# Cross attention in split float32: the weighing that opens a group of four heads moves between two value products

## The chip, the cores and the metric

The kernel runs on one core of a Trainium2 chip (trn2). The metric is the device time of one execution in microseconds (us); less is better. Engines are named as in the profile: PE is TensorE (PEld its weight loads), DVE is VectorE, ACT is ScalarE, POOL is GpSimd, SP is SyncE, which issues most of the DMAs.

## The reference

The model is six residual layers on a sequence x of 256 tokens by 512; the change touches only the first one, a cross attention of 16 heads of width 128 over a context of 4096 tokens:

```
x = x + softmax((LN(x) @ Wq) @ (ctx @ Wk).T / sqrt(128)) @ (ctx @ Wv) @ Wo     # per head, summed over heads
```

The other layers (a self attention, a small expert layer, an attention over the context, a self attention, a mixture of 64 experts) follow it and are the same code before and after.

## The kernel before, in words

Precision. Every float32 operand of the large products is split in two parts: ACT rounds it (`round_*`, a CAST to fp32r), DVE subtracts the rounded part from the original (`split_*`), and PE makes three products (hi by hi, lo by hi, hi by lo). A product's result therefore costs an ACT operation and a DVE operation, in this order, before PE can use it.

Tiling. The 4096 context tokens are 8 chunks (index j) of 512 tokens. A step (h, j) of the loops works on head h and, one head ahead, on head h+1. On PE a step has these pieces:

- K(h+1, j), `project_k`: the keys of chunk j for the next head, 12 matmuls, into bank 0.
- V(u), `project_v`: the values of 128 tokens for four heads at once (a "quad"), 12 matmuls, into one of two banks. Unit u counts all 128-token pieces of all quads; the units of quad g+1 are made during the heads of quad g. `units(h, j)` gives those of a step: none at j=0 and two at j=1 of the head that starts a quad (h = 0, 4, 8, `starts_quad`), one in every other step.
- S(h+1, j), `scores`: scores of the next head, 12 narrower matmuls into the twin bank. It waits for both key parts (`k_split`) and for the copy of the former scores out of the bank (`s_stored`).
- W(h, j), `weigh`: values weighted by the exponentials of chunk j, 8 matmuls. It waits for its values in `v_back` and for both parts of the exponentials (`e_split`). W(h, 7) is carried out in step 0 of the next head and W(h, 0) in step 1, the others one step late (W(h, j-1) at the head of step j).

Values go through DRAM: each V(u) is rounded and split into one buffer `v_out` and spilled by SP (`spill`) to `v_dram`; POOL loads the chunk that a weighing needs into the one buffer `v_back` as soon as the weighing before it is done (`load_v`). For u above 32 `round_v(u)` waits until the spill of unit u-1 has landed, because there is only the one `v_out`. `project_v(u)` waits until unit u-2 is split.

At the start of quads 4 and 8 POOL first issues two loads of the new `wv_parts` (`load_wv`), then the largest score's reduction over partitions, and then the load for W(h, 0).

Order. All engines run in the order written; each list of steps (`tensor_cross`, `scalar_cross`, `vector_cross`, `sync_cross`, `gpsimd_cross`) is written by hand. In step 1 ACT has: round exponentials, copy scores, raise scores, round values; DVE has: split exponentials, running maximum, split values, sum of exponentials. In step 2 DVE has in addition, for h above 0, a reciprocal (`invert_row`).

Late heads (h = 12, 13, 14, from `LATE`) have no value units left. Their loops are separate. In step 6 the weights wk and wq of head h+2 are rounded and split, wk first; `project_q(h+2)` runs at the end of step 7 and `project_k(h+2, 0)` after it.

Of the kernel before, what the change touches and what calls it, by code (L numbers as in the profile page):

```python
# [20 lines left out]
NCH = NKV // CH  # L21
CT = CH // P
XH, XHD = 16, 128
# [40 lines left out]
def build(nc, a, out):  # L64
    ctx = ExitStack()
    with ctx:
# [260 lines left out]
        def units(h, j):  # L327

            if h >= LATE:
                return []  # L330
            s = h % HPQ * NCH + j
            first = (h // HPQ + 1) * KVT
            return [] if s == 0 else [first, first + 1] if s == 1 else [first + s]

        def sync_cross(e):
            def load_qo(n):
                which, h = qo_order[n]
# [78 lines left out]
            for h in range(XH):  # L416
                for j in range(NCH):
                    if j == 0:
                        if h == 0:
                            e.wait_ge(q_projected, 2)  # L420
                            e.wait_ge(*v_spilled(KVT - 1))
                            load_qo(qo_order.index(("wq", 2)))
                        elif h < XH - 1:
                            e.wait_ge(q_projected, h + 2)
                            load_qo(qo_order.index(("wo", h - 1)))
                        if h == XH - 2:
                            e.dma_start(x[:], a["x"]).then_inc(x_in, 16)
                        if not has_halves(h):
                            load_wk(h + 2)
                    if j == 1 and h == XH - 1:  # L430
                        e.wait_ge(y_projected, h)
                        load_qo(qo_order.index(("wo", h)))
                    if j == NCH - 2 and has_halves(h):
                        load_wk(h + 2)
                    for u in units(h, j):
                        spill(u)
                    if j == 5 and 0 < h < XH - 1:
                        e.wait_ge(y_projected, h)
                        load_qo(qo_order.index(("wq", h + 2) if h + 2 < XH else ("wo", h)))
                    if half_at(h, j) is not None:  # L440
                        spill_half(half_at(h, j))
                    if half_at(h, j + 1) is not None:
                        load_half(h, half_at(h, j + 1))

        def tensor_cross(e):
# [135 lines left out]
            for h in range(LATE):  # L581
                for j in range(NCH):
                    if j >= 2:
                        weigh(h, j - 1)
                    elif j == 0 and h and not starts_quad(h):
                        weigh(h - 1, NCH - 1)
                    project_k(h + 1, j)
                    if j == 0 and h and starts_quad(h):
                        weigh(h - 1, NCH - 1)
                    if j == 0 and h == 0 or j == 1 and h:  # L590
                        weigh(h, 0)
                    for u in units(h, j):
                        project_v(u)
                    scores(h + 1, j)
                    if j == NCH // 2 and h:
                        finish_head(h - 1)
                    if j == NCH - 1:
                        project_q(h + 2)
# [20 lines left out]
        def scalar_cross(e):  # L619
# [127 lines left out]
            for h in range(LATE):  # L747
                for j in range(NCH):
                    if j == 0:
                        if h:  # L750
                            store_scores(h, NCH - 1)
                        round_q(h + 1)
                        round_k(h + 1, 0)
                        if h:
                            raise_scores(h, 0)
                            round_e(h, 0)
                        for u in units(h, 0):
                            round_v(u)
                        raise_scores(h, 1)
                        continue  # L760
                    if j == 1:
                        round_k(h + 1, 1)
                    round_e(h, j)
                    store_scores(h + 1, j - 1)
                    if j > 1:
                        round_k(h + 1, j)
                    if j == NCH - 1:
                        round_wk(h + 2)
                    else:
                        raise_scores(h, j + 1)  # L770
                    for u in units(h, j):
                        round_v(u)
                    if half_at(h, j) is not None:
                        round_half(half_at(h, j))
                    if j == 3 and h:
                        round_qo("wo", h - 1)
                        round_o(h - 1)
                    if j == NCH - 2:
                        round_qo("wq", h + 2)
            for h in range(LATE, XH - 1):  # L780
                store_scores(h, NCH - 1)
                round_q(h + 1)
                round_k(h + 1, 0)
                raise_scores(h, 0)
                round_e(h, 0)
                round_k(h + 1, 1)
                raise_scores(h, 1)
                round_e(h, 1)
                store_scores(h + 1, 0)
                for j in range(1, NCH):  # L790
                    if j + 1 < NCH:
                        raise_scores(h, j + 1)
                    if j > 1:
                        store_scores(h + 1, j - 1)
                    if j + 1 < NCH:
                        round_e(h, j + 1)
                        round_k(h + 1, j + 1)
                    if j == 3 and h == LATE:
                        round_qo("wo", h - 1)
                        round_o(h - 1)  # L800
                    if j + 1 == NCH - 1 and h + 2 < XH:
                        round_wk(h + 2)
                        round_qo("wq", h + 2)
            h = XH - 1
            store_scores(h, NCH - 1)
            for m in HALVES:
# [9 lines left out]
        def vector_cross(e):  # L816
# [235 lines left out]
            for h in range(LATE):  # L1052
# [17 lines left out]
                shift(h, 2)  # L1070
                split_e(h, 1)
                keep_max(h + 1, 0)
                for u in units(h, 1):
                    split_v(u)
                sum_e(h, 1)
                if half_at(h, 1) is not None:
# [1 line left out]
                for j in range(2, NCH):  # L1078
                    split_e(h, j)
                    if j == 4 and h:  # L1080
                        split_qo("wo", h - 1)
                        split_o(h - 1)
                    if j in (3, 4, 5):
                        split_k(h + 1, j)
                        shift(h, j + 1)
                    else:
                        if j + 1 < NCH:
                            shift(h, j + 1)
                        split_k(h + 1, j)
                    if j == NCH - 1:  # L1090
                        sum_e(h, j)
                        split_wk(h + 2)
                    keep_max(h + 1, j - 1)
                    for u in units(h, j):
                        split_v(u)
                    if j == 3 and h:
                        scale_o(h - 1)
                    if j < NCH - 1:
                        sum_e(h, j)
                    if half_at(h, j) is not None:  # L1100
                        split_half(half_at(h, j))
                    if j == 2 and h:
                        invert_row(h - 1)
                    if j == NCH - 2:
                        split_qo("wq", h + 2)
            for h in range(LATE, XH - 1):
# [14 lines left out]
                for j in range(1, NCH):  # L1121
                    if j + 2 < NCH:
                        shift(h, j + 2)
                    if j + 1 < NCH:
                        sum_e(h, j + 1)
                    if j in (1, 3, NCH - 2):
                        split_k(h + 1, j + 1)
                    if j == 3 and h == LATE:
                        split_qo("wo", h - 1)
                        split_o(h - 1)  # L1130
                    keep_max(h + 1, j - 1)
                    if j + 1 < NCH:
                        split_e(h, j + 1)
                        if j not in (1, 3, NCH - 2):
                            split_k(h + 1, j + 1)
                    if j == 2:
                        invert_row(h - 1)
                        scale_o(h - 1)
                    if j == 5 and h == XH - 2:
                        add_heads()  # L1140
                    if j + 1 == NCH - 1 and h + 2 < XH:
                        split_wk(h + 2)
                        split_qo("wq", h + 2)
            h = XH - 1
            keep_last_max()
            move_o(h - 1)
# [1562 lines left out]
```

## Time and profile before

| | us |
|---|---|
| median of 3 runs | 1631.89 |
| lowest, highest | 1631.61, 1635.02 |
| the profiled execution | 1632.26 |
| its span | 1630.4 |
| PE busy in it | 1595.6 (98%) |
| DVE busy in it | 1175.9 (72%) |
| ACT busy in it | 728.2 (45%) |

The span is the time from the first to the last instruction of the profiled execution. Busy matmul time counts overlapping matmuls once. A line of the timeline reads: start and duration in us, engine, source line, operation, output<-input, count, and in brackets the idle time before it with what ended it. A matmul of 512 columns follows the one before it after some 0.23 us and shows a duration of 0.39 us, so the length of a piece is best read as the distance between the starts of the first matmuls of it and of the next piece.

### The profile page before, as it was taken

What the parts mean: (1) busy time and instruction counts of PE and PEld (TensorE: products, weight loads), DVE (VectorE), ACT (ScalarE), POOL (GpSimd) and SP (SyncE); (2) the same over time, 40 slices, a digit from 0 to 9 for tenths busy, and PEclk for the clock granted to TensorE, in tenths of its full rate; (3) what the DMA queues carried; (4) which work ended last, traced back from release to release, by engine and by line L of the source; (5) the groups of instructions that cost most, each with busy time, mean ns of one, the idle gap of its engine ahead of it and who ended that gap; (6) DMA issues with size and microseconds to landing.
All of it is one profiled execution on the core that took longest, in us unless ns stands there. A gap on an engine that the chain in (4) does not pass through costs nothing. (4 is left out here: it accounts for less than half of the span.)

```text
span 1630.4 us, 23096 instructions
## 1 busy us (share of the span) xinstructions
PE 1595.6 (98%) x8798; PEld 1255.8 (77%) x8798; DVE 1175.9 (72%) x2127; ACT 728.2 (45%) x981; POOL 192.5 (12%) x247
## 2 busy tenths in 40 slices
PE   9999999999999999989999999998999999999998
PEld 7887888888788888878888888887757757544544
DVE  5555888888788888878888889999583762633333
ACT  4334554555455555544555556565331351322221
POOL 0001011010100101010110101111100071011110
PEclk9999999999999999999999999999999999999999
DMA  7876555564655655554455444334320517489994
GB/s 237 228 228 191 156 148 148 145 162 124 176 145 148 154 144 156 124 167 133 133 135 134 134 120 123 104 116 138 128 102 30 206 52 309 179 262 416 424 423 171
DMA packets 125661, 283.48 MB, mean 174 GB/s; under 512 B 7729, under 2 KB 83697, under 8 KB 119409
## 3 DMA queue, kind: packets, MB, share of 16 engines
q1 hardware_dynamic: 103248, 201.27, 38.1%
q0 software_dynamic: 22304, 80.75, 17.8%
q8 instruction: 70, 1.15, 0.3%
q14 instruction: 39, 0.31, 0.1%
HBM read 207.51 MB, written 74.48 MB: 173 GB/s over the span
## 5 line engine op out<-in xcount | busy, mean ns | idle before, releaser
L502 PE MATMUL bank<-wv_parts,cT_hi 128*128 128x512 f32 x1024 | 334.4, 390 | 1.0 <-DMA wv_parts<-wv_dram 1.0
L502 PEld LDWEIGHTS bank<-wv_parts,cT_hi 128*128 128x128 f32 x1024 | 192.8, 188 | 41.3 <-DMA wv_parts<-wv_dram 1.4
L470 PE MATMUL bank<-cT_hi,wk_hi 128*128 128x512 f32 x512 | 201.2, 393 | 0.6 <-DVE cT_lo L858 0.6
L470 PE MATMUL bank<-cT_lo,wk_hi 128*128 128x512 f32 x512 | 200.0, 391 | 0.0
L502 PE MATMUL bank<-wv_parts,cT_lo 128*128 128x512 f32 x512 | 199.8, 390 | 0.0
L470 PE MATMUL bank<-cT_hi,wk_lo 128*128 128x512 f32 x512 | 199.8, 390 | 0.0
L704 ACT CAST e_parts<-S 128x1024 fp32r<-128x1024 f32 (+1 forms) x129 | 134.9, 1045 | 139.7 <-PE bank L526 133.9
L964 DVE TENSOR_TENSOR e_parts<-S,e_parts 128x1024 fp32r<-128x1024 f32 (+1 forms) x129 | 156.0, 1209 | 40.6 <-ACT e_parts L704 37.7
L695 ACT ACTIVATE S<-S 128x1024 f32<-128x1024 f32 (+1 forms) x129 | 136.0, 1055 | 103.4 <-DVE S L930 101.3
L881 DVE TENSOR_TENSOR mx<-mx,S 128x256 f32<-128x256 f32 x390 | 165.3, 424 | 18.4 <-ACT S L689 8.1
L930 DVE TENSOR_TENSOR S<-S,mrow 128x1024 f32<-128x1024 f32 (+1 forms) x129 | 162.2, 1258 | 4.7 <-POOL mrow L1205 4.6
L953 DVE TENSOR_TENSOR esum<-esum,S 128x256 f32<-128x256 f32 x360 | 152.3, 423 | 9.5
L526 PE MATMUL bank<-e_parts,v_back 128*128 128x512 f32 x424 | 155.3, 400 | 0.0
L1192 POOL DMA_DIRECT2D v_back<-v_dram x110 | 59.0, 537 | 802.2 <-PE bank L526 776.0
L41 PE MATMUL bank<-q_hi,k_hi 128*128 128x256 f32 x512 | 145.6, 284 | 2.6 <-DVE k_lo L865 2.3
L689 ACT COPY S<-bank 128x1024 f32<-128x1024 f32 x128 | 129.3, 1011 | 36.2 <-PE bank L41 21.4
L41 PE MATMUL bank<-q_lo,k_hi 128*128 128x256 f32 x512 | 145.0, 283 | 0.0
L41 PE MATMUL bank<-q_hi,k_lo 128*128 128x256 f32 x512 | 145.0, 283 | 0.0
L673 ACT CAST k_hi<-bank 128x512 fp32r<-128x512 f32 x128 | 75.1, 587 | 151.3 <-PE bank L470 151.2
L865 DVE TENSOR_TENSOR k_lo<-bank,k_hi 128x512 fp32r<-128x512 f32 x128 | 88.2, 689 | 63.9 <-ACT k_hi L673 63.6
L525 PE MATMUL bank<-e_parts,v_back 128*128 128x256 f32 x424 | 121.2, 286 | 0.2
L470 PEld LDWEIGHTS bank<-cT_lo,wk_hi 128*128 128x128 f32 x512 | 96.2, 188 | 21.4
(328 smaller groups left out, 2793.7 us busy)
## 6 DMA issues: line engine op xcount, KB each, us to landing
w<-in_w_moe SPq DMA_DIRECT2D x32, 2304.0 KB, 15.4
v_dram<-v_out SPq DMA_DIRECT2D x112, 512.0 KB, 4.7
v_back<-v_dram POOLq DMA_DIRECT2D x110, 512.0 KB, 4.6
ctx_nat<-in_ctx SPq DMA_DIRECT2D x8, 1024.0 KB, 5.4
ctx_raw<-in_ctxT SPq DMA_DIRECT2D x7, 1024.0 KB, 8.9
v_dram<-v_back SPq DMA_DIRECT2D x14, 512.0 KB, 4.9
v_late<-v_dram POOLq DMA_DIRECT2D x14, 512.0 KB, 3.7
wv_parts<-wv_dram POOLq DMA_DIRECT2D x6, 1024.0 KB, 8.2
```

The costliest lines, as they stand in the source:

```text
L41: last = e.matmul(dst, lhs, rhs, start=(n == 0), stop=(n == len(terms) - 1))
L470: t = e.matmul(banks[b][:], l, r, start=(c == 0 and m == 0), stop=(c == DT - 1 and m == 2))
L502: t = e.matmul(banks[b][:], l, r, start=(c == 0 and m == 0), stop=(c == DT - 1 and m == 2))
L525: e.matmul(*low, start=False, stop=False)
L526: t = e.matmul(*wide, start=False, stop=(j == NCH - 1 and i == CT - 1))
L689: e.copy(S[:, j * CT:(j + 1) * CT, :].rearrange("p a t -> p (a t)"), twin[:]).then_inc(s_stored, 1)
L695: e.activation(Sj, Sj, ACT.Exp).then_inc(raised, 1)
L704: e.copy(e_place(n)[:, 0, of_chunk(0, m), :], S[:, of_chunk(j, m), :]).then_inc(e_rounded, 1)
L881: t = e.tensor_tensor(mx[:], Sj[:, 0] if first else mx[:], Sj[:, i], ALU.max)
L930: e.tensor_tensor(Sj, Sj, mrow[:].unsqueeze(1).to_broadcast([P, CT if m is None else CT // 2, T]), ALU.subtract).then_inc(shifted, 1)
L953: t = e.tensor_tensor(total, l, r, ALU.add)
L964: e.tensor_tensor(lo, S[:, of_chunk(j, m), :], hi.bitcast(F32), ALU.subtract).then_inc(e_split, 1)
```

## The change

Three edits, all in the cross attention.

At quads 4 and 8 (h = 4 and 8) W(h, 0) no longer stands before the two value units of step 1 but between them: K, V(first), W(h, 0), V(first+1), S. At h = 0, where W(0, 0) stands in step 0, the order of PE is unchanged.

At all three quad starts (h = 0, 4, 8) `moved_units` moves the rounding (ACT), the splitting (DVE) and the spill (SP) of the second unit from step 1 to step 2, ahead of those of step 2's own unit. Step 1 has then one unit on these engines and step 2 has two.

In the late heads, wq of head h+2 is rounded and split before wk of it, and in step 6 of h = 14 the last exponentials are split before the running maximum of the scores and not after it.

```diff
+        def moved_units(h, j):
+            if h < LATE and starts_quad(h) and j in (1, 2):
+                pair = units(h, 1)
+                return pair[:1] if j == 1 else pair[1:] + units(h, 2)
+            return units(h, j)
...
 # SP
-                    for u in units(h, j):
+                    for u in moved_units(h, j):
                         spill(u)
...
 # PE
-                    if j == 0 and h == 0 or j == 1 and h:
+                    if j == 0 and h == 0 or j == 1 and h and not starts_quad(h):
                         weigh(h, 0)
-                    for u in units(h, j):
+                    for n, u in enumerate(units(h, j)):
+                        if j == 1 and n == 1 and h:
+                            weigh(h, 0)
                         project_v(u)
...
 # ACT, and DVE in two places (split_v)
-                    for u in units(h, j):
+                    for u in moved_units(h, j):
                         round_v(u)
...
 # ACT, late heads (DVE the same with split_)
                     if j + 1 == NCH - 1 and h + 2 < XH:
+                        round_qo("wq", h + 2)
                         round_wk(h + 2)
-                        round_qo("wq", h + 2)
...
 # DVE, late heads
+                    if j == NCH - 2 and h == XH - 2:
+                        split_e(h, j + 1)
                     keep_max(h + 1, j - 1)
                     if j + 1 < NCH:
-                        split_e(h, j + 1)
+                        if j < NCH - 2 or h < XH - 2:
+                            split_e(h, j + 1)
```

## Rows read from the trace of the kernel before

**Rows 1.** The page, part 1: busy time, share of the span, instructions.
```profile
PE 1595.6 (98%) x8798; PEld 1255.8 (77%) x8798; DVE 1175.9 (72%) x2127; ACT 728.2 (45%) x981; POOL 192.5 (12%) x247
```
**Rows 2.** Waits of PE, 0:1130; waiter <- releaser: total us, times, longest us.
```profile
PE bank L522 <- DMA v_back<-v_dram: 6.2, 2, 3.9
PE bank L540 <- DVE esum_t L981: 3.4, 1, 3.4
...
PE bank L41 <- DVE wqo_lo L848: 1.0, 2, 0.5
...
PE bank L525 <- DVE e_parts L964: 0.6, 1, 0.6
```
**Rows 3.** Timeline of PE at the three quad starts: the idle times.
```profile
160.82 0.39 PE L41 MATMUL bank<-q_hi,k_hi 128*128 128x256 f32 x1 [1.81 <-DVE k_lo L865]
...
424.32 0.50 PE L522 MATMUL bank<-e_parts,v_back 128*128 128x512 f32 x1 [2.25 <-DMA v_back<-v_dram]
...
706.21 0.55 PE L522 MATMUL bank<-e_parts,v_back 128*128 128x512 f32 x1 [3.91 <-DMA v_back<-v_dram]
```
**Rows 4.** Windows: length, busy PE, PEld, DVE, ACT, POOL, PEclk, DMA share, GB/s.
```profile
424.00:426.00 2.00, 1.68 (x9) 1.50 (x10) 1.18 (x2) 0.00 (x0) 0.00 (x0) 1.00 0.00 0
706.00:708.70 2.70, 2.49 (x9) 2.15 (x10) 0.00 (x0) 0.00 (x0) 0.00 (x0) 0.60 0.00 0
...
1128.70:1131.00 2.30, 2.26 (x7) 1.33 (x8) 2.27 (x5) 1.33 (x4) 0.50 (x2) 0.73 0.46 98
```
**Rows 5.** Issue to landing: spills issued at 430.22, 435.29, 510.79; load at 426.31.
```profile
DMA to landing us min/median/max: 3.7/3.7/3.7
...
DMA to landing us min/median/max: 5.6/5.6/5.6
...
DMA to landing us min/median/max: 4.0/4.0/4.0
...
DMA to landing us min/median/max: 3.6/3.6/3.6
```
**Rows 6.** Timeline of PE, head 5, step 1: first matmuls of W, V, S, W.
```profile
496.82 0.39 PE L522 MATMUL bank<-e_parts,v_back 128*128 128x512 f32 x1
...
498.23 0.39 PE L502 MATMUL bank<-wv_parts,cT_hi 128*128 128x512 f32 x1
...
500.95 0.28 PE L41 MATMUL bank<-q_hi,k_hi 128*128 128x256 f32 x1
...
502.38 0.28 PE L525 MATMUL bank<-e_parts,v_back 128*128 128x256 f32 x1
```
**Rows 7.** Timeline of PE: K(5,1)'s last matmul; first of S(1,3), S(5,3), S(9,3).
```profile
421.69 0.39 PE L470 MATMUL bank<-cT_lo,wk_hi 128*128 128x512 f32 x1
...
169.22 0.28 PE L41 MATMUL bank<-q_hi,k_hi 128*128 128x256 f32 x1
...
448.31 0.28 PE L41 MATMUL bank<-q_hi,k_hi 128*128 128x256 f32 x1
...
731.84 0.28 PE L41 MATMUL bank<-q_hi,k_hi 128*128 128x256 f32 x1
```
**Rows 8.** Timeline of ACT, then of DVE, head 4, steps 1 and 2.
```profile
433.95 0.59 ACT L716 CAST v_out<-bank 128x512 fp32r<-128x512 f32 x1 [4.53 <-DMA v_dram<-v_out]
...
439.76 1.79 DVE L881 TENSOR_TENSOR mx<-mx,S 128x256 f32<-128x256 f32 x4
441.62 0.69 DVE L969 TENSOR_TENSOR v_out<-bank,v_out 128x512 fp32r<-128x512 f32 x1
...
443.94 1.75 DVE L988 RECIPROCAL esum_t<-esum_t 128x256 f32<-128x256 f32 x1
...
446.68 0.68 DVE L865 TENSOR_TENSOR k_lo<-bank,k_hi 128x512 fp32r<-128x512 f32 x1
```
**Rows 9.** The page, part 5: the group of key roundings on ACT.
```profile
L673 ACT CAST k_hi<-bank 128x512 fp32r<-128x512 f32 x128 | 75.1, 587 | 151.3 <-PE bank L470 151.2
```
**Rows 10.** Waits of DVE, 985:1128, the late heads.
```profile
DVE S L930 <- POOL mrow L1205: 1.0, 2, 0.6
```

More of the change, by code:

```diff
@@ L1072, in vector_cross @@
                 keep_max(h + 1, 0)
-                for u in units(h, 1):
+                for u in moved_units(h, 1):
                     split_v(u)
@@ L1093, in vector_cross @@
                     keep_max(h + 1, j - 1)
-                    for u in units(h, j):
+                    for u in moved_units(h, j):
                         split_v(u)
@@ L1141, in vector_cross @@
                     if j + 1 == NCH - 1 and h + 2 < XH:
+                        split_qo("wq", h + 2)
                         split_wk(h + 2)
-                        split_qo("wq", h + 2)
             h = XH - 1
```

## The prediction

> **What bounds the kernel now.** I read part 1 of the page first. PE is busy 98% of the span [rows 1], so only what PE stands idle for, or computes slowly, can be won. Next come PE's waits over the cross attention [rows 2]: 6.2 us in two waits for `v_back`, 3.4 us for `esum_t` at the end, 1.0 us in two waits for `wqo_lo`, 0.6 us for `e_parts`. The timeline of PE at the quad starts places the first two: W(4,0) at 424.32 after 2.25 us and W(8,0) at 706.21 after 3.91 us of idleness, and at h=0 S(1,2) waits 1.81 us for `k_lo` [rows 3]. So PE is the bound in heads 0 to 11, except for a few us at each quad start.
>
> The windows show a second cost. After the 3.91 us the granted clock is 0.60, a mixture of the levels 1.2 and 2.4 GHz; after the 2.25 us it is 1.00; after the 3.4 us wait for `esum_t` it is 0.73 [rows 2 to 4]. Idleness of 3.4 us lowered the clock here, 2.25 us did not. The price of one fall is read at h=8: W(8,0) takes 706.21 to 708.69 = 2.48 us against 1.41 us in head 5 [rows 3, 6], and the V behind it some 0.6 us more; 1.6 us in all is my estimate.
>
> The lengths of PE's pieces come from head 5 [rows 6]: W 498.23-496.82 = 1.41, V 500.95-498.23 = 2.72, S 502.38-500.95 = 1.43. K has 12 matmuls of V's shape: 2.72.
>
> **Part 1, W(h,0) between the two V.** PE issues no matmul more or less. At h=4, K(5,1) is issued by 421.69+0.23 = 421.92 [rows 7]. V(64) fills 421.92 to 424.64; the values landed for 424.32, so W(4,0) starts without a wait: 2.4 us less at this point. At h=8 V(96) covers 2.72 us of the wait, and the remaining 1.3 us is under the 2.25 us that left the clock alone; W(8,0) still starts at 706.21, but the V is already done and W runs at full rate. What is pushed back is load (h,1), issued behind W(h,0): 3.6 us to landing [rows 5], against V + S = 4.15 us until W(h,1), minus some 0.5 us to the issue. It just fits, as the same order does in head 5, where W(5,1) starts with no wait [rows 6].
>
> **Part 2, the second unit handled a step later.** This is where the gain can go. `v_out` is one buffer, so between the roundings of two units lies a spill's round trip. Before, it lies in step 1: ACT waits 4.53 us for it at 433.95 [rows 8], while PE has 11 us of work in that step. After, step 1 has one unit and step 2 has two, so the round trip lies in step 2, on ACT and DVE both, since DVE waits for ACT. What stands behind it on DVE is the sum, the reciprocal, the split of the exponentials, and then `k_lo` of K(5,3), for which S(5,3) waits.
>
> At h=4 step by step. PE: W(4,0) 424.64, V(65) 426.05, S(5,1) 428.77, W(4,1) 430.20, K(5,2) 431.61 to 434.33, V(66), S(5,2), W(4,2), K(5,3), V(67) to 445.3. There PE is free for S(5,3), 3 us earlier than its 448.31 before [rows 7]. DVE: `k_hi` of K(5,2) needs 0.2 us to start and 0.59 us [rows 9], so `k_lo` starts at 435.15, the maximum at 435.8, and by the distance 441.62-439.76 = 1.86 us at most (1.72 us of it is work) the split of V(65) at 437.5 and its spill at 438.2 [rows 8]. Landing: 3.7 us alone, 4.0 us where a load follows some 2 us later, 5.6 us where a load runs beside it all the way [rows 5]. Here load (4,3) is issued behind W(4,2), at about 440.4, 2.2 us later, so I take 4.0: V(66) is rounded at 442.2. From a rounding to the end of `k_lo`: 0.62 us to the DVE split, then 441.62 to 446.68+0.68 = 5.74 us [rows 8], 6.36 in all. S(5,3) can start at 448.6. Against 448.31 that is a loss of 0.3 us: the 2.4 us won in front of W(4,0) are gone, and PE now stands idle 3.2 us before S(5,3). Up to 0.2 us more may be lost at the next `k_lo`.
>
> At h=8 the same chain from 706.21 [rows 3]: V(97) 707.62, S 710.34, W 711.77, K(9,2) 713.2 to 715.9; split of V(97) 719.1, spill 719.8, next rounding 723.8, `k_lo` done 730.2. S(9,3) stood at 731.84 [rows 7]: 1.6 us won, with PE free at 727 and 3.2 us idle.
>
> At h=0 PE's order does not change. S(1,2) goes at 158.9 and loses its 1.81 us wait [rows 3]. K(1,2) ends at 156.1, V(33) is split at 159.3, spilled at 160.0, V(34) rounded at 164.0. No reciprocal (1.75 us [rows 8]) stands here, so `k_lo` comes after 6.36-1.7 = 4.7 us by DVE's work; the copy of the scores and `k_hi` [rows 9] in line on ACT make it 5.3. S(1,3) starts at 169.4 against 169.22 [rows 7]: 0.2 us lost, PE idle 2.2 us.
>
> What else moves with the unit: on SP the second spill and, behind step 2's own spill, the load of a weight half for step 3; that load starts about 1.4 us later than before (the split of V(66) goes from 441.62 [rows 8] to 442.9), while ACT takes the half up only some 7 us after its load, so nothing waits. On PE V(67) waits for the split of V(65), done at 438.2, five us before V(67) starts: no cost. POOL's queue is not touched.
>
> Sum of the quads: 0.2+0.3+0.2-1.6 = -0.9 us. The ends: with the 3.7 us landing all three are 0.3 us better (-1.8); with 5.6 us they are 1.6 us worse each (+3.9).
>
> **The clock at the new stalls.** The 3.2 us before S(5,3) and S(9,3) lie between the 2.25 us that kept the clock and the 3.4 us that lost it [rows 2 to 4]; h=0's 2.2 us is like the former. Each fall would cost 1.6 us. With even odds at each, one fall in two is the likeliest count: +1.6 us, ends 0 and +3.2. A rule stands beside this: the Trainium skill, "TensorE: Matmul & The Clock Gate", section "HAM oscillation — how this bites in real kernels", says that a wait for data long enough to make the gate fall is paid twice, in the wait and in a cold start behind it. The trace agrees at 706.21, where the clock is 0.60.
>
> **Part 3, late heads.** wq split ahead of wk gives `wqo_lo` 0.6 us earlier and ends both waits of 0.5 us [rows 2]; wk is 0.6 us later, but PE needs it only after a `project_q` and a W, 3 us on. DVE is the busier engine here; PE's 0.5 us reaches it only through POOL, which issues a load behind W before it starts the maximum: DVE waits 1.0 us for `mrow` in two waits [rows 10]. I take 0.7 us, ends 0 and 1.0. Splitting the last exponentials earlier ends the 0.6 us wait [rows 2], but PE next waits 3.4 us for `esum_t`, at the end of a DVE chain that has the same operations in another order: it waits 4.0 us instead. The clock is down there already [rows 4], so nothing changes: 0, with 0.6 us won as the other end.
>
> **Sum.** -0.9 + 1.6 - 0.7 = 0.0 us. The profiled execution took 1632.26 us, 1.86 us around its span of 1630.4; the median of the runs is 0.37 us below it. I carry the change to the median: 1631.9 us.
>
> **Rivals.**
> *No fall of the clock*: the stalls stay nearer to 2.25 us. Then -1.6 us, 1630.3. For it: the estimate of 3.2 us is below 3.4. *Both fall*: +1.6 us, 1633.5. For it: 3.2 is much nearer to 3.4 than to 2.25.
>
> *The round trip under load* (the slower side). In step 2 the spill of the second unit runs beside a value load and takes 5.6 us, as the one at 435.29 did [rows 5]. Each quad loses 1.6 us more (4.8), the stalls become 4.8, 4.8 and 3.8 us, all above 3.4, and the clock falls three times (4.8): -1.6+4.8+4.8 = +8.0, 1639.9. It decides from a landing of about 4.5 us on. Against it: the load comes 2.2 us after the spill.
>
> *The spill wait hidden* (the faster side): step 2 has enough room on DVE, PE keeps its lead and nothing stands before S(h+1,3). Then h=0 wins 1.8, h=4 2.7, h=8 2.7+0.2+1.6, the late heads 0.7: -9.7, 1622.2. For it: DVE is busy 72% only [rows 1]. Against: the second rounding would have to start 3 us earlier, before the spill it waits for has landed.
>
> **How the numbers follow.** Forecast (one fall) 0.34, no fall 0.24, both 0.20, round trip under load 0.13, spill wait hidden 0.09. A measurement of this kernel tells 0.2%, 3.3 us, from no change. Faster by more: the hidden wait and a margin of the no-fall case (quick landings, late heads at their best) for errors of my chain, 0.15. Slower by more: the loaded round trip and a part of the double fall, 0.18. Within: 0.67. The range takes in the landings between 3.7 and about 4.6 us with none to two falls: 1627.5 to 1636.5.
>
> **What would show it.** Right: no or little idleness before W(4,0), some 1.3 us before W(8,0) with the clock at 1.00 behind it; about 3.2 us of idleness before S(5,3) and S(9,3), 2.2 us before S(1,3), ended by `k_lo`; ACT waiting 4 us or more for `v_out`'s spill in step 2 and not in step 1; no wait for `wqo_lo`; a longer one for `esum_t`. Wrong: no PE wait for `k_lo` in step 3, or `v_back` still late at W(4,0), or a new wait at W(h,1).

## The result and the profile after

| | before | after |
|---|---|---|
| median, us (22 runs each) | 1632.42 | 1636.26 |
| lowest to highest, us | 1629.45 to 1635.44 | 1632.48 to 1640.45 |
| ratio of the times, 95% | | 1.0022 (1.0014 to 1.0029) |
| the profiled execution, us | 1632.26 | 1639.22 |
| its span, us, and mean granted clock | 1630.4, 0.997 | 1637.2, 0.993 |

The changed kernel is slower by 3.8 us of median, 0.14 to 0.29%. That is within my range and 4.4 us above my forecast. The runs of after differ with the clock: five took 1632.5 to 1633.3 us at a mean clock of 0.996, six took 1638.4 to 1640.5 us at 0.992 to 0.994, and the profiled one is of the last group. So its span, 6.8 us over before's, is more than the median's difference, and I read causes from its stretches, not from its total. The recorded mean clocks show how much of the loss goes with the clock: they average 0.9942 over the 22 runs of after and 0.9960 over the 66 runs of before that were timed beside the experiments. That difference times the span is 3 us, my estimate for the clock's part of the 3.8 us.

Part 1 of the page of after, against [rows 1]:

```profile
PE 1600.9 (98%) x8798; PEld 1260.9 (77%) x8798; DVE 1175.9 (72%) x2127; ACT 727.7 (44%) x981; POOL 192.6 (12%) x247
```

PE has the same number of matmuls and is busy 5.3 us longer, which goes with the lower mean clock of this execution (0.993 against 0.997). PE's waits of after over the heads of the cross attention, 0:1134, against [rows 2] (us in total, times, longest):

```profile
PE bank L41 <- DVE k_lo L874: 8.0, 3, 2.9
PE bank L547 <- DVE esum_t L990: 4.4, 1, 4.4
...
PE bank L529 <- DMA v_back<-v_dram: 1.3, 2, 0.9
```

The 6.2 us of waiting for `v_back` are 1.3, the 1.0 us for `wqo_lo` are gone, and the waits for `k_lo` are 8.0 us in three. Before had 2.3 us of them, 1.8 of it in front of S(1,2) [rows 3]; that wait is gone and the three new ones stand one step later. PE's timeline places them. W(4,0) starts with no wait, W(8,0) after 0.89 us, and S(1,3), S(5,3) and S(9,3) start after 2.25, 2.84 and 2.88 us:

```profile
169.61 0.39 PE L41 MATMUL bank<-q_hi,k_hi 128*128 128x256 f32 x1 [2.25 <-DVE k_lo L874]
...
426.60 0.39 PE L529 MATMUL bank<-e_parts,v_back 128*128 128x512 f32 x1
...
450.41 0.39 PE L41 MATMUL bank<-q_hi,k_hi 128*128 128x256 f32 x1 [2.84 <-DVE k_lo L874]
...
710.09 0.50 PE L529 MATMUL bank<-e_parts,v_back 128*128 128x512 f32 x1 [0.89 <-DMA v_back<-v_dram]
...
734.21 0.58 PE L41 MATMUL bank<-q_hi,k_hi 128*128 128x256 f32 x1 [2.88 <-DVE k_lo L874]
```

What those idle stretches did to the clock is in the windows behind them (length; PE, PEld, DVE, ACT, POOL busy; granted clock; DMA share; GB/s). At all three S it fell, and behind W(8,0) it stayed. The last row is a stretch after the cross attention, in code that the change leaves alone:

```profile
169.60:173.90 4.30, 4.29 (x20) 3.92 (x21) 4.13 (x9) 1.83 (x3) 0.00 (x0) 0.65 0.00 0
450.40:454.90 4.50, 4.49 (x21) 4.21 (x22) 4.36 (x9) 2.76 (x5) 0.00 (x0) 0.62 0.03 12
709.00:714.00 5.00, 4.11 (x20) 3.32 (x20) 1.72 (x2) 2.21 (x3) 0.56 (x1) 1.00 0.15 30
734.20:738.60 4.40, 4.39 (x21) 4.20 (x22) 4.26 (x9) 2.46 (x4) 0.00 (x0) 0.63 0.01 4
1165.00:1170.00 5.00, 3.61 (x20) 3.42 (x21) 1.75 (x5) 0.59 (x1) 1.98 (x5) 0.76 0.17 56
```

Before's answer to that last row, at the same place of the program, has the clock at 1.00:

```profile
1160.00:1165.00 5.00, 3.77 (x32) 3.58 (x33) 1.60 (x5) 0.73 (x2) 1.98 (x5) 1.00 0.17 56
```

Behind the waits stands the round trip of `v_out`. ACT and DVE of after in step 2 of head 4, against [rows 8]:

```profile
444.00 0.58 ACT L725 CAST v_out<-bank 128x512 fp32r<-128x512 f32 x1 [5.13 <-DMA v_dram<-v_out]
```

```profile
444.62 0.69 DVE L978 TENSOR_TENSOR v_out<-bank,v_out 128x512 fp32r<-128x512 f32 x1 [4.40 <-ACT v_out L725]
445.22 1.79 DVE L962 TENSOR_TENSOR esum<-esum,S 128x256 f32<-128x256 f32 x4
446.94 1.74 DVE L997 RECIPROCAL esum_t<-esum_t 128x256 f32<-128x256 f32 x1
448.60 1.16 DVE L973 TENSOR_TENSOR e_parts<-S,e_parts 128x1024 fp32r<-128x1024 f32 x1
449.68 0.68 DVE L874 TENSOR_TENSOR k_lo<-bank,k_hi 128x512 fp32r<-128x512 f32 x1
```

DVE stands idle 4.40 us for the second unit's rounding, and then does 5.7 us of work in a row, the last piece of which PE waits for. From the rounding's start to the end of `k_lo` it is 450.36-444.00 = 6.36 us.

**Where the time went.** I took one landmark in each head, the start of the maximum `mrow` on POOL, and behind the heads the layer norms; the difference to before is the running lead (-) or lag (+) in us. The two right columns are two experiments below, "The wait kept, the clock held" and "The gap filled on DVE".

| landmark | before at, us | after | fillers on PE | gap filled on DVE |
|---|---|---|---|---|
| head 1 | 208.01 | +2.03 | +0.11 | -1.06 |
| head 5 | 488.22 | +3.74 | +0.38 | -3.30 |
| head 8 | 695.92 | +4.19 | +0.52 | -3.08 |
| head 9 | 771.75 | +3.92 | -1.54 | -7.39 |
| head 12 | 980.48 | +3.58 | -1.89 | -7.83 |
| head 15 | 1127.71 | +3.13 | -2.23 | -8.14 |
| end of cross attention | 1158.31 | +5.16 | -0.75 | -6.36 |
| next layer | 1216.68 | +6.77 | -0.8 | -4.74 |

The quad starts at h=0 and h=4 cost 2.0 and 3.74-1.96 = 1.8 us (the lag at head 4 is 1.96); h=8 wins 0.3. The 2.0 us at the end of the cross attention hold 1.4 us of a wait for a late `v_tail`:

```profile
PE bank L532 <- DMA v_tail<-v_dram: 1.4, 1, 1.4
```

The last 1.6 us are the fall of the clock at 1165 in unchanged code. Those last two the median carries only in part: it differs by 3.8 us, not 6.8.

Each column is one execution, and executions differ. Three experiments below run before's code up to head 1 (W between alone, the late heads alone, the fillers in the tail of before) and stand there at -0.94, -0.91 and -1.47 us, mostly because before's profile waits 1.81 us in front of S(1,2) and theirs 0.79, 0.80 and 0.94 us. A difference of 1 to 2 us at one landmark can therefore lie between two executions of the same code; the ratios of the times do not have this weakness.

### The profile page after: what moved, and what is told of

Read it like the earlier page. It is cut to its first block, busy times and chain, and to the rows that moved or that the text cites. A ratio compares the mean times of both kernels' runs of the same rounds, so it can differ in the third digit from the quotient of the medians.

```text
span 1637.2 us, 23096 instructions
## 1 busy us (share of the span) xinstructions
PE 1600.9 (98%) x8798; PEld 1260.9 (77%) x8798; DVE 1175.9 (72%) x2127; ACT 727.7 (44%) x981; POOL 192.6 (12%) x247
## 4 chain that ended last, share of the span: by engine, by line
PE 79%; issue 9%; DVE 5%; DMA 3%; ACT 2%; POOL 2%; SPq 0%; DVEq 0%; POOLq 0%; ACTq 0%
PE bank L509 20%; PE bank L41 17%; PE bank L477 16%; PE bank L2356 5%; PE bank L533 5%; PE bank L532 3%; PE bank L2395 2%; PE bank L1922 2%; PE bank L2381 2%; PE bank L1936 1%; PE bank L569 1%; PE bank L2385 1%; DMA v_dram<-v_out 1%; PE bank L2341 1%; DMA wv_parts<-wv_dram 1%
```

## The experiments

After the result my theory was: DVE's chain behind the round trip sets S(h+1,3), as forecast, and every one of the three waits makes the clock fall, at about 1.6 us each, while edit 1 alone (W between the two V) would win. The rivals were that the late heads or edit 1 itself lose the time, and that the round trip suffers from the DMA load. Each kernel was timed 5 to 11 times beside before on the same chip; ratios are against before, with the 95% interval. Edit 1 is the new place of W, edit 2 the second unit handled in step 2.

**The edits one by one.** Three kernels, each before with one part of the change: W(h,0) between the two V; the second unit handled in step 2; the late heads' orders.

```
W between:   - if j == 0 and h == 0 or j == 1 and h:
             + if j == 0 and h == 0 or j == 1 and h and not starts_quad(h):
             + for n, u in enumerate(units(h, j)):
             +     if j == 1 and n == 1 and h: weigh(h, 0)
unit moved:  - for u in units(h, j):          (SP, ACT and DVE)
             + for u in moved_units(h, j):
late heads:  + round_qo("wq", h + 2) / split_qo("wq", h + 2) ahead of wk's; split_e(h, j + 1) of the last step ahead of keep_max
```

> The kernel before with the first edit alone: W(4,0) and W(8,0) between the two value products; rounding, splitting and spill stay where they were, late heads as before. Theory 1 (the round trip of the second unit's spill is what took the gain back, not the new place of W): the wait for v_back falls from 6.2 us to about 1.3 us (only at W(8,0)), the clock stays at 1.00 behind it, the wait for k_lo in step 2 stays small at h=4 and 8 and 1.8 us at h=0; time 1 to 3 us below before, 1630 to 1631. Theory 2 (the place of W costs, by a later load of the next values or a later first rounding): a new wait at W(h,1) or S(h+1,1), time 2 us or more above before.

Measured: 1637.27 us against 1633.08, ratio 1.0025 (1.0015 to 1.0035). The gain of theory 1 did not come. The loss has the size that theory 2 named, but not its wait: none is new at W(h,1) or S(h+1,1). The profile of this kernel has PE's first wait on `k_lo` again, but now in step 2:

```profile
PE bank L41 <- DVE k_lo L867: 8.0, 4, 3.6
...
PE bank L522 <- DMA v_back<-v_dram: 1.7, 2, 1.1
```

PE at S(5,2) and DVE in front of it, then the clock behind:

```profile
439.81 0.58 PE L41 MATMUL bank<-q_hi,k_hi 128*128 128x256 f32 x1 [3.59 <-DVE k_lo L867]
...
434.48 0.69 DVE L971 TENSOR_TENSOR v_out<-bank,v_out 128x512 fp32r<-128x512 f32 x1 [5.19 <-ACT v_out L718]
439.08 0.68 DVE L867 TENSOR_TENSOR k_lo<-bank,k_hi 128x512 fp32r<-128x512 f32 x1
```

```profile
439.80:445.00 5.20, 5.19 (x20) 4.90 (x21) 4.99 (x10) 0.92 (x2) 0.00 (x0) 0.50 0.40 113
```

Before has the same point with no wait:

```profile
439.90 0.39 PE L41 MATMUL bank<-q_hi,k_hi 128*128 128x256 f32 x1
...
439.16 0.68 DVE L865 TENSOR_TENSOR k_lo<-bank,k_hi 128x512 fp32r<-128x512 f32 x1
```

In before `k_lo` ends at 439.84 and S(5,2) starts at 439.90. So PE's 2.25 us in front of W(4,0) were not time to be won: PE and DVE arrived together at S(5,2). Edit 1 alone moves the wait behind the round trip, makes one wait of 3.59 us of it, and the clock goes to 0.50.

About 1 us of that wait is new. Head 4's landmark stands at -1.10 us in this kernel, so S(5,2) comes 1.0 us later than in before when it is measured from there. The reason is on ACT: the second rounding starts 5.9 us after the first one (427.95) and not 5.1 us (428.85 and 433.95 in before), because the spill of V(64) lands after 4.5 us and not 3.7 [rows 5]. What differs around the spill is the load for W(4,1): with the new order it is issued 1.8 us behind the spill (429.3 and 431.1), in before 4.4 us behind it (430.2 and 434.6). After has the new order too, and there this spill also takes 4.5 us. That the load is the cause is my reading; no run moves the load alone, and the spill at 510.79 took 4.0 us with a load 1.8 us behind it.

```profile
433.86 0.59 ACT L718 CAST v_out<-bank 128x512 fp32r<-128x512 f32 x1 [5.34 <-DMA v_dram<-v_out]
```

```profile
DMA to landing us min/median/max: 4.5/4.5/4.5
```

> The kernel before with the second edit alone: rounding, splitting and spill of the second unit in step 2, PE's order and the late heads as before. Theory 1: step 2 gets the round trip while PE has no lead: S(5,3) and S(9,3) some 2.8 us later than in before (splitting of V(65) at 440.0, spill 440.7, V(66) rounded 444.7, k_lo done 451.1 against S at 448.31), S(1,3) 0.2 us later, PE idle 2 to 3 us before each and the clock falls there: 8 to 11 us above before, 1641 to 1643. Theory 2 (the moving is harmless, the new place of W costs): within 1 us of before.

Measured: 1642.47 against 1633.08, ratio 1.0064 (1.0050 to 1.0078), as expected. This kernel has both kinds of waits:

```profile
PE bank L41 <- DVE k_lo L872: 8.1, 4, 2.9
PE bank L529 <- DMA v_back<-v_dram: 6.4, 3, 3.5
```

Either edit alone loses, edit 2 by 0.64%. Together they lose 0.22%, about what edit 1 loses alone (0.25%, the intervals overlap): once edit 1 is in, edit 2 neither costs nor wins until DVE's order is changed too.

> The kernel before with the edits of the late heads alone (wq ahead of wk, last exponentials ahead of the maximum). Theory 1: both waits for wqo_lo gone, the wait for esum_t longer by 0.6 us, time 0.3 to 1.0 us below before: not told from before. Theory 3 (the loss sits in the tail: the longer wait for esum_t, then a slower PE and a value load that collides with the next layer's weights): 1.5 us or more above before.

Measured: 1632.86 against 1633.08, ratio 1.0001 (0.9992 to 1.0010): not told from before. Its waits for `wqo_lo` are gone and the one for `esum_t` is 4.4 us instead of 3.4. In its profile the running lead grows by 0.40 us over the late heads (-1.66 at head 12, -2.06 at head 15), in after by 0.45.

**The gap filled on DVE.** If the chain is the cause, work that DVE does anyway and that `k_lo` does not need can go into the 4.4 us in which DVE waits for the second rounding. The sum and the reciprocal are such work (1.79 and 1.74 us). Kernel: after, with this in DVE's order:

```
+ filled = j == 2 and starts_quad(h)
  for n, u in enumerate(moved_units(h, j)):
      split_v(u)
+     if filled and n == 0:
+         sum_e(h, j)
+         if h: invert_row(h - 1)
- if j < NCH - 1:
+ if j < NCH - 1 and not filled:      (and invert_row likewise)
```

> The changed kernel, with DVE's sum of exponentials and reciprocal of step 2 at the three quad starts carried out between the splits of the two units, in the 5 us in which DVE waits for the spill. Theory 1 (what stands behind the round trip on DVE is what PE waits for): k_lo of step 3 comes 2.8 us earlier at h=4 and 8 and 1.7 us at h=0; PE's wait there falls from 2.2 to 2.9 us to under 0.6 us and the clock stays up in all three places: 9 to 12 us below the changed kernel, 1624 to 1628, faster than before too. Theory 4 (ACT's chain or the DMA alone sets k_lo, or the clock falls for another reason): the wait for k_lo stays over 2 us, or falls and the time stays within 2 us of the changed kernel.

Measured: 1626.84 us against 1633.08, ratio 0.9961 (0.9947 to 0.9975), inside the expected range. DVE's rows in step 2 of head 4, to be read against those of after above:

```profile
437.13 1.80 DVE L962 TENSOR_TENSOR esum<-esum,S 128x256 f32<-128x256 f32 x4
438.84 1.75 DVE L997 RECIPROCAL esum_t<-esum_t 128x256 f32<-128x256 f32 x1
441.62 0.69 DVE L978 TENSOR_TENSOR v_out<-bank,v_out 128x512 fp32r<-128x512 f32 x1 [1.03 <-ACT v_out L725]
...
443.97 0.69 DVE L874 TENSOR_TENSOR k_lo<-bank,k_hi 128x512 fp32r<-128x512 f32 x1 [0.17 <-ACT k_hi L682]
```

The wait for the rounding is 1.03 us and not 4.40; `k_lo` starts 2.3 us after the split of the second unit, not 5.1 us. PE then finds it nearly ready, and the clock stays:

```profile
444.71 0.39 PE L41 MATMUL bank<-q_hi,k_hi 128*128 128x256 f32 x1 [0.16 <-DVE k_lo L874]
```

```profile
444.60:449.00 4.40, 4.29 (x26) 3.89 (x27) 4.26 (x10) 2.89 (x6) 0.53 (x1) 1.00 0.21 51
```

By the table it is 7.4 us ahead of before at head 9 and 8.1 us at head 15, and gives 1.8 us back by the end of the cross attention, where the 4.4 us wait for `esum_t` stands unchanged.

**The wait kept, the clock held.** To part the wait from the clock, this kernel is after with seven small matmuls on PE in front of S(h+1,3), into a bank whose content is not used; the wait for `k_lo` remains.

```
+ if j == 3 and starts_quad(h):
+     e.wait_ge(s_stored, (h + 1) * NCH + j)
+     stay_awake(e, twin, 7)
  scores(h + 1, j)
```

> The changed kernel, with seven small matmuls on PE ahead of S(1,3), S(5,3) and S(9,3), as soon as the former scores are out of the bank: they fall into the idle time in front of k_lo and take nothing from anyone. Theory 1 (half of the loss is the clock, which falls in each of the three new stalls): the wait for k_lo is cut to under 1 us at a time, the clock behind it stays at 1.00, k_lo comes when it came, and the time falls by 3 to 5 us, to 1631 to 1633. Theory 5 (the clock's falls cost nothing, since DVE is behind anyway): the time stays within 1 us of the changed kernel, 1635.5 to 1637.

Measured: 1631.16 us against 1631.93, ratio 0.9992 (0.9983 to 1.0001). PE in front of S(5,3), and the windows behind S(5,3) and S(9,3):

```profile
446.18 1.83 PE L137 MATMUL bank<-ident 128*128 128x128 f32 x14 [0.51 <-ACT S L701]
448.40 0.39 PE L41 MATMUL bank<-q_hi,k_hi 128*128 128x256 f32 x1 [0.38 <-DVE k_lo L877]
```

```profile
448.40:452.90 4.50, 4.50 (x27) 4.06 (x28) 4.36 (x9) 3.10 (x6) 0.53 (x1) 1.00 0.04 12
731.00:736.00 5.00, 5.00 (x29) 4.33 (x28) 4.79 (x12) 3.69 (x6) 0.53 (x1) 1.00 0.32 71
```

The same chain, the same start of S(5,3) (448.40; the forecast said 448.6), the clock at 1.00. It is 0.30% or 4.9 us better than after by the two ratios: 1.6 us for each of three falls. By the table the landmarks give 2.03-0.11 = 1.9 us at h=0, 1.4 us more at h=4 (by the lags at heads 4 and 5), and 1.8 us more at h=8. The mean clocks agree: 0.9972 over the 11 runs with fillers against 0.9942, which times the span is 4.9 us too. This is the experiment that shows the clock as the cause of after's loss: with the clock held, the change takes as long as before does or 1 us less.

**With the gap filled, is edit 1 still needed?** The kernel of the filled gap with edit 1 taken back:

```
- if j == 0 and h == 0 or j == 1 and h and not starts_quad(h):
+ if j == 0 and h == 0 or j == 1 and h:
-     if j == 1 and n == 1 and h: weigh(h, 0)
```

> The version with the sum and the reciprocal in the gap of step 2 (6.2 us below before), but with W(4,0) and W(8,0) ahead of both value products as in before: only the first edit taken back. Theory 1 (the new place of W is worth its 2.4 us at h=4 and 2.7 + 1.6 us at h=8 as soon as DVE no longer holds PE back): the wait for v_back is back at 5.5 to 6.4 us with the fall of the clock at h=8, time 5 to 7 us above that version, 1631 to 1634. Theory 2 (the place of W does not matter, all of the gain is DVE's order): within 1.5 us of it, 1625.5 to 1628.5.

Measured: 1631.65 against 1631.93, ratio 1.0003 (0.9994 to 1.0012), in the expected range. `v_back` is waited for again:

```profile
PE bank L529 <- DMA v_back<-v_dram: 6.6, 3, 3.6
```

Against the filled gap with edit 1 it is 0.42%, 6.9 us, worse, the falls of the clock at W(4,0) and W(8,0) included; the expectation was 5 to 7. By the landmarks 3.8 us of it come at h=4 and 4.0 us at h=8. So W's place between the two V is worth some 7 us once DVE is quick enough; while DVE's chain was the limit, it was worth nothing.

**Edit 1 with the gap filled, but no moved unit.** The kernel with edit 1 alone, and the sum of step 1 put between its two splits:

```
  for n, u in enumerate(units(h, 1)):
      split_v(u)
+     if n == 0 and starts_quad(h):
+         sum_e(h, 1)
```

> W between the two value products and the sum of exponentials of step 1 between the splits of the two units, which stay in step 1; late heads as before. Theory 1: what stands behind the round trip on DVE is 1.8 us shorter, so the 3.6 and 3.5 us waits for k_lo of step 2 in the version with W between alone fall to 1.8 us, the clock stays up: 5 to 7 us below that version, 1630 to 1632; a little behind the version that moves the second unit (1626.8), because the split of e_parts and the shift still stand behind the round trip. Theory 4 (the spill's landing alone sets it): the waits stay at 3 us or more and the time within 2 us of 1637.

Measured: 1628.38 against 1631.93, ratio 0.9980 (0.9971 to 0.9989), better than expected. The waits for `k_lo` in front of S(5,2) and S(9,2) are 2.48 and 1.75 us and the clock behind both is 1.00; all waits for `k_lo` halved, from 8.0 us to

```profile
PE bank L41 <- DVE k_lo L867: 4.2, 2, 2.5
```

The order of DVE's work in the gap turns edit 1 from a loss of 0.25% into a gain of 0.20%, without moving a unit.

**Edit 1 with the clock held.** Edit 1 alone and six small matmuls in front of S(h+1,2) at quad starts:

```
+ if j == 2 and starts_quad(h):
+     e.wait_ge(s_stored, (h + 1) * NCH + j)
+     stay_awake(e, twin, 6)
```

> The version with W between the two value products alone (4.2 us above before, PE waits 3.6 and 3.5 us for k_lo of step 2), with six small matmuls on PE ahead of S(1,2), S(5,2) and S(9,2), as soon as the former scores are out of the bank. Theory 1 (the first edit alone lost by the clock, not by its place): clock 1.00 behind the waits, S(5,2) and S(9,2) where they were, 4 to 6 us below the version without them, 1631 to 1633, a little below before. Theory 2 (the place of W costs by itself): 1635 or more.

Measured: 1634.16 against 1632.26, ratio 1.0008 (0.9999 to 1.0017), between what the two theories named. The clock did stay:

```profile
440.00:446.00 6.00, 5.89 (x33) 5.22 (x34) 5.79 (x12) 2.98 (x4) 0.54 (x1) 1.00 0.41 108
```

and S(5,2) started at 440.11, not earlier than in before (439.90). Against edit 1 alone this is 0.17%, some 2.8 us, better, and not the 4 to 6 us expected; against before edit 1 wins nothing even so. That agrees with the reading that PE's earlier arrival meets DVE at the same point. The last 1 us over before is not the clock's: the mean clocks are 0.9963 over these 11 runs and 0.9960 in before's. The slower spill seen above is here too (a landing of 4.5 us, the second rounding 6.0 us after the first, S(5,2) 1.1 us later than in before from a head 4 at -0.88 us) and has the right size, but no run takes it away alone.

**The tail.** The 4.4 us wait for `esum_t` also lowers the clock. The filled-gap kernel's window behind it:

```profile
1122.00:1125.00 3.00, 3.00 (x4) 1.01 (x3) 2.77 (x6) 2.82 (x5) 0.00 (x0) 0.50 0.49 158
```

One kernel puts 16 small matmuls into this wait on top of the filled gap, another 12 of them on before alone:

```
  weigh(h - 1, NCH - 1)
+ stay_awake(e, banks[K_BANK], 16)
  finish_head(h - 1)
```

> The version with the sum and reciprocal in the gap of step 2, with 16 small matmuls on PE in the 4.4 us before the last sums of head 14 (behind the last W of head 14), where the clock falls in before and after. Theory 1 (a fall there costs PE's next 5 us some 1.5 us on the path): clock 1.00 behind the wait, 1 to 2 us below the version without them, 1625 to 1626. Theory 5 (DVE and ACT set the pace of the last head, so the fall costs nothing): within 0.5 us of 1626.8.

Measured: 1623.08 us (1619.78 to 1625.01) against 1631.93, ratio 0.9947 (0.9934 to 0.9961), 0.14% below the filled gap alone. With five runs each the two intervals overlap, so the times alone do not show this gain; the mean clocks do not overlap, 0.998 to 1.000 in these runs and 0.995 to 0.997 without the fillers, and 1.000 in the profiled execution. The same stretch there:

```profile
1118.00:1121.00 3.00, 2.51 (x11) 1.59 (x12) 2.96 (x6) 2.04 (x4) 0.95 (x2) 1.00 0.39 127
```

> The kernel before, with 12 small matmuls on PE in the 3.4 us before the last sums of head 14 and nothing else. Theory 1: the fall of the clock there (0.73 in before's window) is gone; in the version with the gap filled, the same step brought about 2.3 us by the two ratios, so 1.5 to 2.5 us below before, 1629.5 to 1630.5. Theory 5 (it counted there only because the wait was 4.4 us and the value loads of the last head lay differently): within 0.7 us of before.

Measured: 1632.76 against 1632.26, ratio 0.9997 (0.9988 to 1.0006): the expected 1.5 to 2.5 us did not come. The clock stayed where the fillers are, and fell later in code that is the same in both kernels:

```profile
1128.00:1134.00 6.00, 5.55 (x33) 4.39 (x34) 5.49 (x9) 4.86 (x8) 0.91 (x2) 1.00 0.47 134
1159.00:1164.00 5.00, 3.65 (x20) 3.46 (x21) 1.72 (x5) 0.59 (x1) 1.98 (x5) 0.74 0.18 52
```

The fillers do what they should in their place. Part of the 11 runs shows a gain: the four at a mean clock of 0.998 took 1629.86 to 1632.05 us, the six at 0.996 took 1632.24 to 1633.55, and the profiled one is of the latter. It has falls that before's profile does not have, behind W(4,0) at 422.72 (0.67 over 4 us) and the one at 1159. Whether the fillers bring other falls on or these would have come anyway is open. So is whether the step wins more on the filled gap than on before: the two gains, 0.14% and 0.03%, are each within their noise.

## Why the prediction was right, and where it was wrong

**Part 1, W(h,0) between the two V.** Right in what it described: no wait at W(4,0), 0.89 us at W(8,0) (forecast 1.3), the clock at 1.00 behind it, 5.3 us of the waits at W(4,0) and W(8,0) gone, no new wait at W(h,1). The forecast said that the 2.4 us won there are gone again by S(5,3), and they were. The edit alone showed that the meeting point was near in before already: S(5,2) stood 0.06 us behind the end of `k_lo`.

**Part 2, the second unit a step later.** Right, and to a few tenths. The landing of the spill of V(65) was 3.7 us (forecast 4.0), with the load issued 2.3 us behind it; at h=0 and h=8 the spill in the same place took 4.1 and 3.7 us. That is the end of the rival with the round trip under load (a landing of 4.5 us or more). The distance from the rounding to the end of `k_lo` was forecast at 6.36 us and measured at 6.36; at h=0 it was forecast at 5.3 and measured at 5.35. Taking each head's own lag out, S(1,3) came 0.4 us later than before (forecast 0.2), S(5,3) 450.41-1.96-448.31 = 0.1 (forecast 0.3) and S(9,3) 734.21-4.19-731.84 = -1.8 (forecast -1.6). The stalls were 2.25, 2.84 and 2.88 us for 2.2, 3.2 and 3.2. With the clock held, the landmarks are at -1.5 us in head 9 and -2.2 in head 15; the forecast had -0.9 for the quads and -0.7 for the late heads. The times say it without the scatter of single profiles: the ratio with fillers is 1.3 us below before (2.8 below to 0.2 above), and the forecast without a fall was 1.6 below. So the step-by-step sum without the clock stands within 0.6 us; that it does so head by head is partly luck, given differences of 1 to 2 us between executions.

**The clock at the new stalls: the step that failed.** I took one fall in two at h=4 and h=8, +1.6 us, and none at h=0, "like the former", because 2.25 us of idleness had kept the clock at 424.32 [rows 3, 4]. All three fell: 0.65, 0.62 and 0.63. Two falls more at 1.6 us are 3.2 us, and 1631.9+3.2 = 1635.1 against the median of 1636.26. The price was right (1.6 us by the times, 1.4 to 1.9 by landmarks, forecast 1.6), the count was not. The same length, 2.25 us, kept the clock in before and lost it in after. A length of idleness alone does not decide it, and my line between two observed lengths had one case on each side.

Both cases were also one execution. The kernel with the late heads alone runs before's code here, and in its profile they come out the other way round: the clock fell behind 2.20 us at W(4,0) and stayed up behind 3.43 us at W(8,0).

```profile
423.23 0.50 PE L529 MATMUL bank<-e_parts,v_back 128*128 128x512 f32 x1 [2.20 <-DMA v_back<-v_dram]
...
706.46 0.50 PE L529 MATMUL bank<-e_parts,v_back 128*128 128x512 f32 x1 [3.43 <-DMA v_back<-v_dram]
```

```profile
423.20:427.20 4.00, 3.97 (x14) 3.27 (x15) 2.12 (x3) 2.26 (x3) 0.56 (x1) 0.70 0.17 28
706.40:710.40 4.00, 3.94 (x19) 3.35 (x20) 1.15 (x2) 2.23 (x3) 0.56 (x1) 1.00 0.19 30
```

At W(4,0) the other three kernels with before's order of PE fell too: to 0.67 over 4 us behind 2.25 us (fillers in the tail of before), to 0.67 behind 2.21 us (the gap filled, edit 1 taken back) and to 0.62 behind 2.08 us (edit 2 alone). So before's profile is the only one of five that kept the clock there. The other way round, edit 2 alone kept it at 1.00 behind 2.87 us in front of S(9,3), and edit 1 with the sum in the gap behind 2.48 us in front of S(5,2). Between 2.1 and 3.4 us these profiles have both outcomes, and the even odds that I gave to 3.2 us fit them better than the certainty that I gave to 2.2 us.

I had also priced "both fall" at 1633.5 us and left the case of three falls without a chance of its own, except inside the loaded round trip. The rule of the Trainium skill, "TensorE: Matmul & The Clock Gate", section "HAM oscillation — how this bites in real kernels", that a stall long enough to lower the gate is paid twice, holds at all three stalls of after (0.65, 0.62 and 0.63 behind them); which stall is long enough is the part that I misjudged.

**Part 3, late heads.** The waits for `wqo_lo` went as said, but the gain is 0.4 to 0.45 us in the profiles and not 0.7, and the part alone can't be told from before (1.0001). The wait for `esum_t` is 4.4 us, forecast 4.0. "The clock is down there already, so nothing changes" is not borne out: over the 8 us behind the wait the clock is 0.79 in before and 0.68 in after, 0.9 us more of it lost.

```profile
1128.70:1136.70 8.00, 7.96 (x39) 5.99 (x40) 7.44 (x10) 5.57 (x9) 0.50 (x2) 0.79 0.35 98
```

```profile
1131.80:1139.80 8.00, 7.92 (x33) 5.72 (x34) 7.47 (x10) 5.43 (x8) 0.54 (x2) 0.68 0.33 98
```

The longer wait need not be the reason. Edit 1 alone waits 3.47 us there, like before, and has 0.59 over the same 8 us. After falls 2.0 us further behind across that stretch, 1.4 us of it the wait for `v_tail`, while the kernel with the late edits alone lost no time that could be measured. Of the 1.2 us between 1635.1 and the median, 0.5 us is the start of the sum: I carried the change to the median of 3 runs, 1631.9, and 22 runs of before give 1632.42. The rest stays open between the tail and falls elsewhere that come in some runs only.

**Rivals.** Of the rivals, "both fall" came nearest: its mechanism with one fall more. The hidden spill wait did not happen (S(h+1,3) waited). Its condition was that the second rounding start 3 us earlier; the filled-gap kernel shows that shortening DVE's work behind it does instead, and wins 6.2 us of the rival's 9.7.

## What to carry to other kernels

When one engine gets ahead of another, look for the next point at which they meet: here PE's 2.25 us at the load were slack behind DVE's round trip, and removing them alone made one longer stall with a lower clock behind it, and the spill whose landing counts took 0.8 us more. Where an engine waits for a buffer's round trip, put into the wait the work that the next consumer does not need; this took the change from +0.22% to -0.39% (with fillers in one more wait -0.53%, a step within the noise of five runs). Price a stall on PE of 2 us or more as its length plus, at some odds, a fall of the clock (1.6 us here), even when a stall of the same length was harmless in one profile; before calling it harmless, look at the same stall in a second execution.

## What the runs showed of the hardware

The granted clock fell at 169.61 in after behind 2.25 us of idleness and stayed at 1.00 at 424.32 in before behind the same 2.25 us. At that place of before's order it fell in four other profiles, behind 2.08 to 2.25 us, and at W(8,0) it stayed up once behind 3.43 us. In edit 1 alone it fell to 0.50 behind 3.59 us. Seven small matmuls (fourteen records) in 1.83 us, inside a stretch of 2.7 us without other work, kept it at 1.00. Falls differ from run to run of one kernel: after ran at a mean clock of 0.996 in some runs and 0.992 in others, 1632.5 to 1640.5 us, and single profiles show a fall at 1159 or 1165 in code that was the same in all kernels. So a profile may hold a fall or two more or less than the median run, at 1.6 us each. Spills of 512 KB landed after 3.7 us with a load of the same size issued 2.3 or 4.4 us behind them, after 4.0 and 4.5 us with one 1.8 us behind them, and after 5.6 us with one issued 0.7 us ahead.
